# An attention layer on one core: one half job in every step, x's turns behind the jobs in a max bank, h's tanh some steps later

## What is computed

```
xn = layer_norm(x, norm_w, norm_b)
q, k, v = xn @ q_w + q_b, xn @ k_w + k_b, xn @ v_w + v_b     # 16 heads of 16
att = softmax(q k^T + mask)                                   # per head, 512 x 512
y = att @ v
scale, shift = split(silu(cond) @ emb_w + emb_b)
h = layer_norm(y, sb_norm_w, sb_norm_b) * (1 + scale) + shift
out = x + silu(h) @ out_w + out_b
```

## Time and profile before

| | |
|---|---|
| median of 3 runs | 539.11 us (538.86 to 539.15) |
| profiled execution | 539.28 us |
| its span | 537.6 us |
| PE busy | 511.4 us, 95% |
| DVE busy | 414.8 us, 77% |
| ACT busy | 351.0 us, 65% |
| POOL busy | 225.4 us, 42% |
| chain that ended last | PE 74%, ACT 9%, issue 8%, POOL 4%, DVE 2% |

### The profile page before, as it was taken

How to read it: one execution, slowest core, us unless ns; L and a number is a source line. 1 busy time by engine, 2 the same in 40 slices (tenths; PEclk the granted TensorE clock), 3 DMA queues, 4 the chain that set the end, 5 groups by cost and what they waited for, 6 DMA issues and landing times.

```text
span 537.6 us, 10041 instructions
## 1 busy us (share of the span) xinstructions
PE 511.4 (95%) x2843; PEld 192.0 (36%) x2843; DVE 414.8 (77%) x661; ACT 351.0 (65%) x645; POOL 225.4 (42%) x270
## 2 busy tenths in 40 slices
PE   7798999899999999999999999999999999988987
PEld 3443333233334333433333333433333333422334
DVE  6587779877887878877887878878787877877625
ACT  2214777677776777677776777677776777566761
POOL 4535323536436443436336443536336443234011
PEclk9988999999999999999999999999999999999999
DMA  5643224343425334253425334253435332252021
GB/s 128 228 120 95 88 86 131 88 128 86 136 84 157 110 106 117 59 170 96 130 87 168 94 105 117 78 157 92 128 88 167 91 98 83 79 158 57 20 60 40
DMA packets 55050, 57.95 MB, mean 108 GB/s; under 512 B 12376, under 2 KB 42200, under 8 KB 55024
## 3 DMA queue, kind: packets, MB, share of 16 engines
q1 hardware_dynamic: 54480, 56.84, 35.8%
q10 hardware_dynamic: 544, 0.79, 0.5%
HBM read 36.35 MB, written 21.00 MB: 107 GB/s over the span
## 4 chain that ended last, share of the span: by engine, by line
PE 74%; ACT 9%; issue 8%; POOL 4%; DVE 2%; SPq 1%; DMA 1%; ACTq 0%; POOLq 0%; DVEq 0%
PE pv_ps L547 21%; PE st_ps L528 19%; PE mx_ps L496 11%; PE job_ps L585 7%; ACT probs L684 6%; PE job_ps L605 5%; PE job_ps L592 5%; PE mx_ps L630 3%; PE mx_ps L506 2%; ACT h_tanh L734 1%; DVE negmax L862 1%; PE mx_ps L635 1%; SPq L1233 1%; DMA vb_row<-in_L_cond_v_b 1%; POOL qk_parts L1135 0%
## 5 line engine op out<-in xcount | busy, mean ns | idle before, releaser
L862 DVE TENSOR_REDUCE negmax<-mx_ps 128x2 f32<-128x1024 f32 x256 | 303.4, 1220 | 86.9 <-PE mx_ps L496 85.9
L684 ACT ACTIVATE probs<-st_ps 128x512 f32<-128x512 f32 x502 | 273.3, 600 | 126.6 <-PE st_ps L528 126.0
L528 PE MATMUL st_ps<-q_rows,k_rows 115*128 115x512 bf16 x502 | 158.1, 385 | 6.1 <-ACT probs L684 3.4
L547 PE MATMUL pv_ps<-probs,v_rows 128*32 128x512 f32 x1024 | 136.4, 605 | 0.6 <-ACT probs L684 0.6
L496 PE MATMUL mx_ps<-k_rows,q_rows 51*128 51x512 bf16 x512 | 79.3, 383 | 6.4 <-DMA k_rows<-qk_dram 4.6
L1135 POOL TENSOR_TENSOR qk_parts<-qk_rest,qk_parts 128x512 bf16<-128x512 f32 x31 | 36.0, 1161 | 102.0 <-DVE qk_parts L936 102.0
L528 PEld LDWEIGHTS st_ps<-q_rows,k_rows 115*128 115x128 bf16 x502 | 38.7, 97 | 110.0 <-ACT probs L684 77.7
L1120 POOL TENSOR_TENSOR qk_parts<-qk_full,zero 128x512 bf16<-128x512 f32 x29 | 32.0, 1103 | 98.8 <-ACT qk_full L706 98.8
L585 PE MATMUL job_ps<-x_norm_t,w_qk 128*128 128x512 f32 x116 | 59.3, 604 | 0.0
L496 PEld LDWEIGHTS mx_ps<-k_rows,q_rows 51*128 51x128 bf16 x512 | 15.7, 94 | 112.4 <-issue 54.2
L1126 POOL TENSOR_TENSOR qk_rest<-qk_full,qk_parts 128x512 f32<-128x512 f32 x31 | 35.9, 1158 | 9.4 <-ACT qk_parts L698 7.1
(11 more groups left out here) (116 smaller groups left out, 401.1 us busy)
## 6 DMA issues: line engine op xcount, KB each, us to landing
qk_dram<-qk_parts SPq DMA_DIRECT2D x128, 128.0 KB
q_rows<-qk_dram SPq DMA_DIRECT2D x124, 96.0 KB
k_rows<-qk_dram SPq DMA_DIRECT2D x124, 96.0 KB
x_in<-in_x SPq DMA_DIRECT2D x16, 256.0 KB, 3.0
x_res<-in_x SPq DMA_DIRECT2D x8, 512.0 KB, 3.9
out<-out_sb SPq DMA_DIRECT2D x16, 256.0 KB, 2.7
w_e<-in_L_cond_emb_w SPq DMA_DIRECT2D x1, 1024.0 KB, 5.7
k_rows<-mask_dram SPq DMA_DIRECT2D x64, 6.0 KB
```

Source lines behind the costliest of these rows:

```text
L528: pe.matmul(st_bank(b, t, h), k_rows[0:ROWS_ALL, g, h, c * P:(c + 1) * P], q_rows[0:ROWS_ALL, g, h, :], start=True, stop=True).then_inc(st ...
L547: mm = pe.matmul(pv_ps[VW * h:VW * (h + 1), :], v_rows[:, c, g * GH + h, :], probs[:, t % P_SLOTS, h, :], start=(c == 0), stop=(c == CH - ...
L684: act.activation(probs[:, t % P_SLOTS, h, :], st_bank(b, t, h), ACT.Exp).then_inc(exp_done, 1)
L862: dve.tensor_reduce(by_pair[:, :, j, c], mx_ps[j][:, :, :], AXIS_X, ALU.max, negate=True).then_inc(max_done, 1)
```

## The change

The last projection (proj 3) is split over the end of one body and the start of the next: A in step 15, Z in step 0. The second output projection moves from step 15 to steps 1 and 2 of the next body. So each of the 16 steps holds half a job. The turns of x leave job_ps and become sides of steps 0 and 2, into mx_ps[0][:, 0], behind the step's job; ACT reads them from there. The side "hturn" 1 moves from step 11 to step 10. The tanh of h moves from steps 8 and 12 on ACT to steps 9 and 11 (TANH: step of the tanh, step of its side). DVE's h_t 0 moves from (8, 2) to (9, 2); h_t 1 stays at (12, 2). In body -1, proj 3 A comes in step 15. On SP the second output store is issued one body later, behind `spread(b, 3, 0)`, and the load of x_res follows it.

```diff
 JOBS = {
-    0: ("proj", 3, 0, AZ), 1: ("xturn", 0, 1, AZ), 2: ("xturn", 1, 1, AZ),
+    0: ("proj", 3, 0, Z), 1: ("outp", 1, -2, A), 2: ("outp", 1, -2, Z),
...
-    15: ("outp", 1, -1, AZ),
+    15: ("proj", 3, 1, A),
 }
...
-SIDE = {1: ("yturn", 3, -1), 5: ("yturn", 0, 0), 7: ("hturn", 0, -1), 9: ("yturn", 1, 0),
-        11: ("hturn", 1, -1), 13: ("yturn", 2, 0)}
-
-LAST_JOBS = {0: ("proj", 3, 0, AZ), 9: ("outp", 0, -1, A), 10: ("outp", 0, -1, Z), 11: ("outp", 1, -1, A),
-             12: ("outp", 1, -1, Z)}
+              6: ("proj", 1, 1, AZ), 7: ("vproj", 1, 1, AZ), 8: ("proj", 2, 1, AZ), 15: ("proj", 3, 1, A)}
+
+SIDE = {0: ("xturn", 0, 1), 1: ("yturn", 3, -1), 2: ("xturn", 1, 1), 5: ("yturn", 0, 0), 7: ("hturn", 0, -1),
+        9: ("yturn", 1, 0), 10: ("hturn", 1, -1), 13: ("yturn", 2, 0)}
+
+LAST_JOBS = {0: ("proj", 3, 0, Z), 1: ("outp", 1, -2, A), 2: ("outp", 1, -2, Z), 9: ("outp", 0, -1, A),
+             10: ("outp", 0, -1, Z), 11: ("outp", 1, -1, A), 12: ("outp", 1, -1, Z)}
...
+TANH = {9: 7, 11: 10}
+LAST_TANH = {7: 6, 8: 7}
...
-LATE = {(1, 2): ("proj", 3, 0), (6, 1): ("proj", 0, 1), (8, 2): ("hturn", 0, -1), (10, 1): ("proj", 1, 1),
+LATE = {(1, 2): ("proj", 3, 0), (6, 1): ("proj", 0, 1), (9, 2): ("hturn", 0, -1), (10, 1): ("proj", 1, 1),
         (12, 2): ("hturn", 1, -1), (14, 1): ("proj", 2, 1)}
...
+            def turn_x(ps, i, d):
+
+                pe.wait_ge(x_norm_ready, CH * (d + 1))
+                for c in range(CH):
+                    mm = pe.transpose(ps[:, c * P:(c + 1) * P], x_norm[:, c, i * P:(i + 1) * P], ident[:, :])
+                return mm
...
+            def read_xturn(ps, i, d):
+
+                act.wait_ge(turned["xturn"], KD * d + i + 1)
+
+                wait(act, turned["proj"], NG * d)
+                act.activation(x_norm_t[:, i, :], ps, ACT.Identity, bias=nb_col[:, i:i + 1],
+                               scale=nw_col[:, i:i + 1]).then_inc(xt_ready, 1)
...
+            def tanh_of_h(b, t):
+
+                of = of_loop(b, {}, TANH, LAST_TANH)
+                if t not in of or not side_at(b, of[t]):
+                    return
+                _, i, d = side_at(b, of[t])
+                act.wait_ge(h_lin_ready, KD * d + i + 1)
+                act.activation(h_tanh[:, i, :], h_lin[:, i, :], ACT.Tanh).then_inc(h_tanh_ready, 1)
...
                     read_job(b, t - 1, 1)
-                    read_side(b, t - 1, 1)
+                    tanh_of_h(b, t)
...
+            def save_out(d, i):
+
+                wait_apart(sp, maskp_ready, out_ready, 2 * d + i + 1)
+                sp.dma_start(batch_of(out_dram, d)[:, 2 * i:2 * i + 2, :], out_sb[:, 2 * i:2 * i + 2, :]
+                             ).then_inc(out_saved, 16)
+
             def body(b):
+                spread(b, 3, 0)
+                if exists(b - 2) and not last_body(b):
+                    save_out(b - 2, 1)
                 if exists(b - 1):
 
                     wait_apart(sp, maskp_ready, out_ready, 2 * (b - 1))
                     sp.dma_start(x_res[:, :, :], batch_of(x_dram, b - 1)).then_inc(res_loaded, 16)
-                spread(b, 3, 0)
                 spread(b, 0, 1)
```

More of the change, by code:

```diff
@@ L142, in side_at @@
         b, step = b - 1, step + STEPS
-    return work_at(of_loop(b, SIDE, SIDE, LAST_SIDE), b, step)
+    return work_at(of_loop(b, {}, SIDE, LAST_SIDE), b, step)
 def late_at(b, step, place):
@@ L363, in attention_layer @@
                     ("vproj", 0): mx_ps[1][:, 0, :], ("proj", 1): mx_ps[1][:, 1, :], ("vproj", 1): job_ps[:, :],
-                    ("proj", 2): st_ps[0][:, :]}
+                    ("proj", 2): st_ps[0][:, :], ("proj", 3): job_ps[:, :]}
         def job_bank(kind, i, b):
@@ L372, in bank_freed @@
             if isinstance(b, int) and b == -1:
-                return {7: (xt_ready, 1), 8: (mask_col_ready, 1)}.get(t)
+                return {7: (xt_ready, 1), 8: (mask_col_ready, 1), 15: (v_plain_ready, 2)}.get(t)
             if 0 not in job_at(b, t)[3]:
@@ L594, in job @@
                 elif kind == "xturn":
-                    pe.wait_ge(x_norm_ready, CH * (d + 1))
-                    for c in range(CH):
-                        mm = pe.transpose(ps[:, c * P:(c + 1) * P], x_norm[:, c, i * P:(i + 1) * P], ident[:, :])
+                    turn_x(ps, i, d).then_inc(turned["xturn"], 1)
+                    return
                 else:
@@ L630, in side @@
                         mm = pe.transpose(ps[:, c * P:(c + 1) * P], y_t[:, c * P:(c + 1) * P], ident[:, :])
+                elif kind == "xturn":
+                    mm = turn_x(ps, i, d)
                 else:
@@ L707, in read_job @@
                 elif kind == "xturn":
[L708 to L712, removed]
+                    read_xturn(ps, i, d)
                 elif kind == "vproj":
@@ L718, in read_job, with read_side @@
                              ).then_inc(v_plain_ready, 1)
-            def read_side(b, t, half):
-                if not side_at(b, t) or side_at(b, t)[0] != "hturn":
+            def read_xturn(ps, i, d):
[3 more added lines that the diff above has]
+                               scale=nw_col[:, i:i + 1]).then_inc(xt_ready, 1)
+            def read_side(b, t):
+                if not side_at(b, t):
                     return
-                _, i, d = side_at(b, t)
-                if half == 0:
+                kind, i, d = side_at(b, t)
+                if kind == "xturn":
+                    read_xturn(mx_ps[0][:, 0, :], i, d)
+                elif kind == "hturn":
                     act.wait_ge(turned["hturn"], KD * d + i + 1)
@@ L731, in read_side @@
                                    scale=mod_now[:, 0, i:i + 1]).then_inc(h_lin_ready, 1)
-                else:
-                    act.wait_ge(h_lin_ready, KD * d + i + 1)
-                    act.activation(h_tanh[:, i, :], h_lin[:, i, :], ACT.Tanh).then_inc(h_tanh_ready, 1)
+            def tanh_of_h(b, t):
+                of = of_loop(b, {}, TANH, LAST_TANH)
+                if t not in of or not side_at(b, of[t]):
+                    return
+                _, i, d = side_at(b, of[t])
+                act.wait_ge(h_lin_ready, KD * d + i + 1)
+                act.activation(h_tanh[:, i, :], h_lin[:, i, :], ACT.Tanh).then_inc(h_tanh_ready, 1)
             def fill_half(i):
@@ L770, in body @@
                     read_job(b, t, 0)
-                    read_side(b, t, 0)
+                    read_side(b, t)
                 if isinstance(b, int) and b == -1:
@@ L1301, in body @@
                 spread(b, 2, 1)
[L1302 to L1306, removed]
+                if exists(b - 1):
+                    save_out(b - 1, 0)
+                    if isinstance(b, int) and b >= B - 1:
+                        save_out(b - 1, 1)
             run(sp, body, B - 2)
```

1 line of the change is left out of this document (removed).

## The result

The changed kernel takes 535.75 us (median of 4 runs, 535.24 to 536.14), against 539.13 (538.86 to 539.34) before: ratio 0.9929, 95% interval 0.9918 to 0.9941. It is faster by 3.4 us. The forecast was 533.0, a gain of 6.1.

A forecast was written before the change was run, and what follows sets the result against it. PE, busy 95% of the span, was taken as the bound. Gains of 5.0 (bodies 1 to 6), 0.8 (body 7) and 0.3 (body 0) made 6.1, giving 533.0 us; the 8-in-10 range was 529.0 to 536.0.

The forecast's parts named there:

- the forecast's own 531.3 to 534.7: Whole kernel: range from body 0's bounds, 0.2 a body for DVE in step 3 and 0.2 at the split; chance 0.55.
- the rival that x's turn stalls: Steps 1 and 3: PE waits up to 0.43 each behind ACT's read; 538.2, or 535.6 at half price; chance 0.20.
- The gain of the middle: Bodies 1 to 6: each shorter by 0.84, 5.0 in all.
- Jobs, 0.87 a body: Steps 15, 0, 1, 2 of a middle body: 16.08 falls to 15.21 with half a job in each step.
- Tanh, nothing: Steps 8 to 14: 0.36 won in step 8, 0.39 lost in step 10, 0 from steps 12 to 14; together +0.03.
- The working at the split: Step 10: h_t 0 delays DVE's split to 264.25, so PE's second max pair goes at 264.42, not 264.03; 0.39 lost.
- six equal bodies: Bodies 1 to 6: the same gain of 0.84 counted for each, 5.0 together.
- The rule of the Trainium skill: Steps 8 and 12: optimize engines blocking the critical path; the tanh's gain is kept, 4.5 more, 528.5; chance 0.17.
- Rows late: Group 0's row loads behind the output store and x_res: 2.85 lost in each of six bodies, time 550; chance 0.05.
- Body 0, 0.3 won: Start of body 0: 0.7 won in step 0, 0.4 lost in step 2, net 0.3.
- the 0.7 forecast: Body 0, step 0: half its 3.12 job leaves, x's turn comes in; 0.7 won, at most 1.56, at least 0.
- the 0.4: Body 0, step 2: gets a side it didn't have as a job, 3.42 to 3.80; 0.4 lost.

The follow-up runs named there:

- e1: Changed kernel with the tanh of h back in steps 8 and 12, hturn 1 in step 11, h_t 0 at (8, 2); jobs stay spread: 535.66 us.
- e6: Kernel before with the tanh part alone (tanh in steps 9 and 11, hturn 1 in step 10, h_t 0 at (9, 2)): 539.82 us, ratio 1.0005.
- e5: Changed kernel with h_t 0 on DVE moved from (9, 2) to (10, 2), behind step 10's reductions: 532.59 us.
- e9: Changed kernel with h_t 0 at (10, 2) and h_t 1 at (12, 0), ahead of step 12's reductions: 530.88 us.
- e10: Changed kernel, but POOL's first operation on head group 3's q and k in body 0 waits for DVE's whole embedding table: 532.96 us.
- e4: Changed kernel with the two tensor_scalar operations for mod_full written as scalar_tensor_tensor, same values: 535.22 us.
- e2: Changed kernel, but body 0's first pv product waits only for DVE's reads of pv_ps, not for the embedding table: 533.60 us.
- e7: As e2, with the embedding's six other operations moved behind DVE's reductions of step 2 in body 0: 533.21 us.
- e3: Changed kernel with proj 3 whole in step 0 of body 0 and no job in step 15 of body -1: 534.17 us.

## Why the prediction was right and wrong

**The number: in the range, by luck.** 535.75 lies within 529.0 to 536.0, but outside the forecast's own 531.3 to 534.7. The range reached that far only to take in a part of the rival that x's turn stalls (535.6 at half its price), and that didn't happen. The gain of the middle came as forecast; the loss came at the start of body 0, which no rival had.

**Jobs, 0.87 a body: right.** Steps 15, 0, 1 and 2 took 3.43 + 3.83 + 4.07 + 3.94 = 15.27 for a forecast 15.21, a gain of 0.82 for 0.87. Nothing of the rival that x's turn stalls as a side: steps 1 and 3 are unchanged. e1 shows that this part carries the whole gain.

**Tanh, nothing: right, and shown twice** (e1, e6). 0.36 won in step 8 and 0.35 in step 12, 0.39 lost in step 10 and 0.36 in step 13. (The working at the split has a slip: 264.25 and the 0.2 of step 2 make 264.45, a loss of 0.42 and not 0.39; 0.39 is what was measured.) The forecast had six equal bodies; in body 6, without statistics, the 0.3 of step 12 was kept, and that made up for the 0.06 a body that the others fell short. e5 and e9 show the mechanism: move h_t 0 off the split's way and the 0.39 is back, move h_t 1 ahead of the reductions and the 0.38 is. The rule of the Trainium skill that the prediction weighed (Perfetto Trace Analysis, "Optimization Strategies") would have had the wait on ACT come back in full; the trace shows 0.71 won and 0.75 paid elsewhere. ACT was the last of two releasers, and DVE the next. POOL has a part in this DVE chain as well. Between h_t 1 and the reductions of step 13 stands a tensor_scalar on 4 values a partition, which takes 0.17 in the fill at 6.31, with POOL idle, and here 0.59, up to the end of POOL's operation:

```profile
274.58 1.42 POOL L1144 TENSOR_TENSOR qk_parts<-qk_full,zero 128x512 bf16<-128x512 f32 x1 [4.05 <-ACT qk_full L718]
...
275.43 0.59 DVE L900 TENSOR_SCALAR x_negmean<-x_mv 128x4 f32<-128x4 f32 x1
```

It takes 0.59 in bodies 1 to 5 of either kernel. Some 0.4 of a DVE chain on which step 13 hangs may be won there (estimate, 0.59 - 0.17); no run tried it.

**Rows late: no.** x_res takes 4.7 to land, for 3.9, but PE's only wait for k_rows in the changed kernel is that of the first fill. The cover for group 3's rows did shrink, which I hadn't looked at: in a middle body the last load is issued 4.36 before PE's max products of step 2, where it was 5.56, and in body 7 3.87. In e1's profile a slow store left 2.69 there, and PE waited 0.59. None of the other profiles has such a wait.

**Body 0, 0.3 won: the step that failed**, in the words of the prediction: "In its place comes a turn of x, and the table of the embedding that DVE makes bounds the next step. I take 0.7 won (estimate; at most 3.12/2 = 1.56, at least 0)". It measured 2.34 lost. I had named the right bound, DVE's table, but gave no cost to anything that lengthens it (1.50 before, 3.12 now), and put the lower end at 0. The upper end, half of 3.12, came from a job at the lower clock; at the upper one half a job is 0.86. That half a job less on PE lets qk_full land earlier, and with it POOL's two operations of 1.04 and 1.15 beside the table, I did not follow. e10 shows the size: with POOL kept away, step 1 starts 1.05 earlier than before (48.61 for 49.66) for the 0.7 forecast, step 2 costs 0.42 for the 0.4, and the kernel takes 532.96 where 533.0 had been forecast. The loss comes apart, in the profiled executions, as 1.45 for the hold-up, 1.52 for the clock behind it, less that 0.63 won. The first is shown by e10; that the clock fell because of the hold-up is not shown. And part of the 1.05 is that PE's clock was low in step 0 before the change and isn't in e10.

**What stays open** is when the clock falls. In the profiles of e1, e4 and e9 it doesn't fall at the start of body 0, with the same idle time of PE (2.08 to 2.09) as in those of the changed kernel and e5 (2.06, 2.08), where it does. What differs is an earlier fall, which every kernel has in the fill of body -1. Windows from 22 to 34 us, e4 and then the changed kernel:

```profile
22.00:26.00 4.00, 1.26 (x6) 0.39 (x4) 1.23 (x10) 1.16 (x2) 1.80 (x4) 0.96 0.50 170
26.00:30.00 4.00, 2.65 (x9) 0.72 (x9) 2.41 (x3) 0.69 (x1) 3.24 (x5) 0.50 0.48 134
30.00:34.00 4.00, 4.00 (x21) 1.73 (x21) 2.74 (x3) 0.00 (x0) 1.18 (x2) 0.68 0.24 62
```

```profile
22.00:26.00 4.00, 2.40 (x13) 0.94 (x11) 2.36 (x13) 1.16 (x2) 3.05 (x5) 1.00 0.51 172
26.00:30.00 4.00, 2.78 (x9) 0.72 (x9) 2.53 (x3) 0.69 (x1) 3.24 (x5) 0.65 0.50 134
30.00:34.00 4.00, 4.00 (x25) 1.97 (x24) 3.14 (x4) 0.00 (x0) 1.02 (x2) 0.92 0.19 60
```

With the early and longer fall step 1 starts at 50.51 to 50.89, with the later and shorter one at 50.06 to 50.19 and the second fall, which costs 1.5, follows. So an early fall gives back only a part of what the later one costs: e4's span is 0.7 shorter than the changed kernel's. This is read from single profiles; e2 fell with no idle time longer than 0.93, the kernel before fell in step 0, and what decides it wasn't settled. It also shifts medians: the executions of one kernel lie up to 3.0 (e7) and 4.1 (e6) apart, so sizes below 1 us are read here from step lengths.

## What to carry to other kernels

The last releaser of a wait is not the wait's price. Before work is taken off it, write down when the next one, here DVE with a strict order of its own, would have let go; then move both, as e9 does. And when a change makes an engine early, follow what its result starts on other engines: here half a job moved away from PE started POOL over 1 us earlier (49.10 in e3, 47.36 and 48.01 in the changed kernel and e1), on top of the one small DVE chain for which PE was waiting.

## What the runs showed of the hardware

- A DVE operation of 0.23 us took 0.89 and 1.18 beside POOL's additions on 128x512 f32, up to their ends, and one of 0.17 took 0.59. DVE's reductions, which read PSUM, kept to 1.22 in the same kernel, and emb_t, which reads PSUM too, ran 0.14 beside POOL and took the 0.62 that it takes in e10 without POOL.
- TensorE's clock is not the same from one execution of a kernel to the next: its mean was 0.990 or 0.994 in the four of the changed kernel, 0.990 to 0.997 in the six of e1. The 7 us at 1.2 GHz cost 1.5 (steps 1 and 2 took 9.44 for 7.92), nearly half of the change's gain of 3.4.
